# A spectral stage in a metaformer kernel: 33 of 64 frequency columns, four image pairs written out, loads placed ahead

## The reference

```python
x_proj = einsum('bchw,mc->bmhw', layernorm_over_channels(x), w_in)      # 16 channels
x_fft = fftshift(fft2(x_proj, norm='ortho'))
mag = abs(x_fft) + 1e-8
gain = einsum('ahw,cahw->chw', angle_weights, bin_weights[:, :, radius_idx])
enh = mag * gain * (cos(angle(x_fft)) + 1j * sin(angle(x_fft)))
x_enh = real(ifft2(ifftshift(enh), norm='ortho'))
x = x + layernorm_over_channels(x) + einsum('bmhw,cm->bchw', x_enh, w_out)
```

## Time and profile before

| what | value |
|---|---|
| median of 3 runs | 3474.5 us |
| lowest and highest | 3469.59 and 3474.97 us |
| the profiled execution | 3470.55 us |
| its span, first to last instruction | 3468.8 us |
| mean granted TensorE clock | 0.91 of full speed |
| TensorE / VectorE / ScalarE / GpSimd busy | 88% / 50% / 44% / 25% of the span |

### The profile page before, as it was taken

How to read it: one execution, slowest core, us unless ns; L and a number is a source line. 1 busy time by engine, 2 the same in 40 slices (tenths; PEclk the granted TensorE clock), 3 DMA queues, 4 the chain that set the end, 5 groups by cost and what they waited for, 6 DMA issues and landing times. The chain is left out here.

```text
span 3468.8 us, 66009 instructions
## 1 busy us (share of the span) xinstructions
PE 3045.2 (88%) x26432; PEld 1701.1 (49%) x26432; DVE 1727.8 (50%) x2317; ACT 1512.8 (44%) x2263; POOL 853.9 (25%) x694
## 2 busy tenths in 40 slices
PE   6766683899999975999998769999999999999989
PEld 1166321455555532566666234646454554646455
DVE  6724286577766440111111254656465555555575
ACT  4412351567677751111222344535454554545434
POOL 3500350344444421111110103121221213121322
PEclk7668675999999985999999789999999999999999
DMA  4611675123433324677777344655645564646244
GB/s 178 237 25 24 217 282 205 67 109 146 155 146 150 150 116 130 186 214 213 208 212 243 113 155 149 208 168 175 205 166 196 164 213 141 234 146 226 100 149 161
DMA packets 233863, 579.59 MB, mean 167 GB/s; under 512 B 38444, under 2 KB 105260, under 8 KB 225068
## 3 DMA queue, kind: packets, MB, share of 16 engines
q1 hardware_dynamic: 233684, 577.26, 49.8%
HBM read 384.24 MB, written 192.94 MB: 166 GB/s over the span
## 5 line engine op out<-in xcount | busy, mean ns | idle before, releaser
L2137 DVE TENSOR_TENSOR d_hid_scaled<-d_hid_scaled,d_gate 128x512 f32<-128x512 f32 x512 | 403.0, 799 | 437.1 <-PE d_ps L1835 266.2
L1835 PE MATMUL d_ps<-d_hid_scaled,d_w 128*128 128x512 f32 x1024 | 525.6, 595 | 4.3 <-DVE d_hid_scaled L2137 4.3
L1533 PE MATMUL c_ps<-c_pad,c_weight 32*32 32x512 f32 x13824 | 474.8, 601 | 26.1 <-ACT c_pad L1485 18.6
L2004 ACT ACTIVATE d_hid_scaled<-d_ps,d_b 128x512 f32<-128x512 f32 x512 | 349.7, 687 | 329.1 <-PE d_ps L1823 322.3
L1533 PEld LDWEIGHTS c_ps<-c_pad,c_weight 32*32 32x32 f32 x13824 | 287.0, 103 | 213.7 <-issue 129.4
L1821 PE MATMUL d_ps<-d_tnh,d_w1h 128*128 128x512 f32 x512 | 318.7, 623 | 19.8 <-ACT d_hid_scaled L2004 19.1
L1164 PE MATMUL b_ps<-b_hid,b_w2s 128*128 128x512 f32 x512 | 260.5, 593 | 0.0
L2089 POOL CAST d_tnh<-d_TN 128x512 fp32r<-128x512 f32 x64 | 47.3, 739 | 857.9 <-PE d_ps L1823 820.6
L1594 DVE COPY c_pad<-c_P 128x1024 f32<-128x1024 f32 x48 | 33.4, 696 | 414.5 <-PE c_ps L1533 379.2
L1485 ACT ACTIVATE c_pad<-c_P 128x1024 f32<-128x1024 f32 x48 | 51.8, 1079 | 392.2 <-PE c_ps L1533 372.0
L1835 PEld LDWEIGHTS d_ps<-d_hid_scaled,d_w 128*128 128x128 f32 x1024 | 194.4, 190 | 51.9 <-DVE d_hid_scaled L2137 5.7
(11 more groups left out here) (259 smaller groups left out, 5671.2 us busy)
## 6 DMA issues: line engine op xcount, KB each, us to landing
d_gate<-scratch_gates SPq DMA_DIRECT2D x256, 512.0 KB, 4.6
scratch_qkv<-b_qkv SPq DMA_DIRECT2D x64, 768.0 KB, 3.5
c_P<-scratch_qkv SPq DMA_DIRECT2D x192, 256.0 KB, 4.7
scratch_agg<-c_out SPq DMA_DIRECT2D x192, 256.0 KB, 4.9
d_buf<-scratch_qkv SPq DMA_DIRECT2D x96, 512.0 KB, 4.1
d_buf<-scratch_agg SPq DMA_DIRECT2D x96, 512.0 KB, 4.1
p_X<-in_x SPq DMA_DIRECT2D x8, 2048.0 KB, 8.4
scratch_s<-p_X SPq DMA_DIRECT2D x8, 2048.0 KB, 6.4
```

What stands on the lines that cost most here:

```text
L1533: end = nc.tensor.matmul(ps[on(i), k * QUADS + h, :].rearrange("p (b r w) -> p b r w", b=2, w=HB), weight[k][on(q), 2 * r + x, on(h)], pad ...
L1835: nc.tensor.matmul(moe_bank(n // E), w2[:, e, :], scaled[n % 3][:, :], start=False, stop=(e == E - 1)).then_inc(moe_pe, 1)
L2004: nc.scalar.activation(hid[n % 3][:, :], hid_bank(n), ACT.Gelu, bias=b1[:, n % E:n % E + 1]).then_inc(hid_done, 1)
L2137: nc.vector.tensor_tensor(scaled[n % 3][:, :], hid[n % 3][:, :], gate[k][:, n % 2 * CH:(n % 2 + 1) * CH], ALU.mult).then_inc(scaled_done, 1)
```

## The change

The spectrum of a real image is symmetric, so the column transform now makes 33 of the 64 columns (`KX`), the factors are computed for 33, and the last table of the inverse counts every column but the first and the last twice. The mask is made symmetric on the host to match. The transforms, and the copies `rows`, `back` and `image`, are cut into halves of 8 channels (`q`), with a wait for each half. The hardware loops are gone: the four pairs are written out. All four pairs of projections are loaded at the start of the stage, into four buffers; there are two image buffers. The gain matmuls come first in the stage. The tables are loaded in `phase_project`, behind the first four image loads.

```diff
+KX = SIDE // 2 + 1
+DFT_TABLES = ((0, 128), (128, 194), (194, 260), (260, 388), (388, 516), (516, 580), (580, 644))
...
@@ phase_project, SP, after the loads of images 0 to 3 @@
+                dft, mask, binw = early
+                for h in range(2):
+                    sp.dma_start(dft[h * SIDE:(h + 1) * SIDE, :], d["dft"]).then_inc(early_loaded, 16)
+                sp.dma_start(mask[:, :], d["mask"]).then_inc(early_loaded, 16)
+                sp.dma_start(binw[:, :], d["binw"]).then_inc(early_loaded, 16)
...
@@ phase_dft, SP @@
+                for i in range(STEPS):
                     for h in range(2):
-                        sp.dma_start(proj[h * SIDE:(h + 1) * SIDE, :, :],
-                                     d["pm"][bass.ds(i * 2 + h, 1), :, :].rearrange("a m (h w) -> h (a m) w", w=SIDE)).then_inc(pm_loaded, 16)
-                with sp.Fori(0, STEPS - 1) as i:
-                    sp.wait_ge(rows_pe, i + 1)
-                    load(i + 1)
-                    store(i)
-                store(STEPS - 1)
+                        sp.dma_start(proj[i][h * SIDE:(h + 1) * SIDE, :, :],
+                                     d["pm"][i * 2 + h:i * 2 + h + 1, :, :].rearrange("a m (h w) -> h (a m) w", w=SIDE)).then_inc(rest_loaded if i else first_loaded, 16)
+                for i in range(STEPS):
+                    sp.wait_ge(image_ready, i * 2 + 2)
...
@@ phase_dft, TensorE @@
-                    stage(high, 128, rows, [(g2a, 0), (g2b, SIDE)]).then_inc(freq_pe, 1)
+                    stage(high[:, q * 2 * CH:(q + 1) * 2 * CH], 128, rows, q, [(g2a, 0), (g2b, SIDE)]).then_inc(freq_pe, 1)
-                    stage(low, 128, enh, [(g3a, 0), (g3b, SIDE)]).then_inc(back_pe, 1)
+                    stage(wide(q), 128, enh, q, [(g3a, 0), (g3b, KX)], cols=KX).then_inc(back_pe, 1)
-                    stage(low, SIDE, back, [(g4a, 0), (g4b, SIDE)]).then_inc(image_pe, 1)
+                    stage(wide(q), SIDE, back, q, [(g4a, 0), (g4b, SIDE)], rows=KX).then_inc(image_pe, 1)
...
+                for i in range(STEPS):
+                    if i + 1 < STEPS:
+                        for q in range(2):
+                            by_columns(i + 1, q)
+                    for q in range(2):
+                        to_lines(i, q)
+                    for q in range(2):
+                        to_image(i, q)
+                    if i + 2 < STEPS:
+                        for q in range(2):
+                            by_rows(i + 2, q)
...
@@ phase_dft, ScalarE @@
+                copy_rows(0)
+                squares(0)
+                magnitude(0)
+                copy_rows(1)
+                for i in range(STEPS):
+                    if i + 1 < STEPS:
+                        squares(i + 1)
+                    copy_back(i, 0)
+                    if i + 1 < STEPS:
+                        magnitude(i + 1)
+                    copy_back(i, 1)
+                    for q in range(2):
+                        copy_image(i, q)
+                    if i + 2 < STEPS:
+                        copy_rows(i + 2)
```

More of the change, by code:

```diff
@@ L565, in _, with phase_dft @@
                 scale(B - 1, range(NCH))
-def phase_dft(nc, d, passed):
+def phase_dft(nc, d, tables):
+    dft, mask, binw = tables
     with ExitStack() as ctx:
@@ L577, in phase_dft @@
         low, high = ps[:, 0:4 * CH], ps[:, 4 * CH:8 * CH]
[L578 to L583, removed]
+        STEPS, HALF = B // 2, MID // 2
+        gain = sb("gain", [128, MID, KX])
+        proj = [sb(f"proj{i}", [128, MID, SIDE]) for i in range(STEPS)]
+        image = [sb(f"image{k}", [128, MID, SIDE]) for k in range(2)]
+        rows, back = [sb(n, [128, MID, 128]) for n in ("rows", "back")]
+        enh, sqz = [sb(n, [128, MID, 2 * KX]) for n in ("enh", "sqz")]
+        r2, mag, zero, den, rec, num, fac, shifted = [sb(n, [128, MID, KX]) for n in
                                                       ("r2", "mag", "zero", "den", "rec", "num", "fac", "shifted")]
[L585 to L588, removed]
+        g1, g2a, g2b, g3a, g3b, g4a, g4b = DFT_TABLES
+        first_loaded, rest_loaded, xe_stored = sem("first_loaded"), sem("rest_loaded"), [sem(f"xe_stored{k}") for k in range(2)]
         rows_pe, rows_ready, freq_pe, sqz_done, r2_done, mag_done, enh_ready = [sem(n) for n in
@@ L623, in _, with stage @@
+                for k in range(2):
+                    sp.wait_ge(xe_stored[k], STEPS // 2 * 32)
             @block.tensor
             def _(pe):
[L625 to L631, removed]
+                def stage(dst, width, src, q, tables, rows=SIDE, cols=SIDE):
+                    for m in range(HALF):
+                        for t, (g, first) in enumerate(tables):
@@ L644, in by_columns @@
-                def by_columns(i):
-                    pe.wait_ge(rows_ready, i + 1)
+                                on = slice(h * SIDE, h * SIDE + rows)
+                                last = nc.tensor.matmul(dst[h * SIDE:h * SIDE + cols, m * width:m * width + g[1] - g[0]],
+                                                        src[on, q * HALF + m, first:first + cols], dft[on, g[0]:g[1]],
+                                                        start=(t == 0), stop=(t == len(tables) - 1))
@@ new lines, in stage, with by_rows @@
+                    return last
+                def by_rows(i, q):
+                    if i == 0:
+                        pe.wait_ge(first_loaded, 32)
+                    else:
+                        pe.wait_ge(rest_loaded, (STEPS - 1) * 32)
+                    if i == 1:
+                        pe.wait_ge(rows_ready, q + 1)
+                    if i >= 2:
+                        pe.wait_ge(image_ready, (i - 2) * 2 + q + 1)
+                    stage(wide(q), 128, proj[i], q, [(g1, 0)]).then_inc(rows_pe, 1)
@@ L661, in _ @@
                 for h in range(2):
-                    for kx in range(SIDE):
+                    for kx in range(KX):
                         last = nc.tensor.matmul(high[h * SIDE:(h + 1) * SIDE, kx * MID:(kx + 1) * MID],
                                                 mask[:, kx * SIDE:(kx + 1) * SIDE], binw[:, :], start=True, stop=True)
[L665 to L671, removed]
@@ L672, in _ @@
-                inverse(STEPS - 1)
+                last.then_inc(rows_pe, 1)
+                for i in range(2):
+                    for q in range(2):
+                        by_rows(i, q)
+                    if i == 0:
+                        for q in range(2):
+                            by_columns(0, q)
+                for i in range(STEPS):
[7 more added lines that the diff above has]
+                    if i + 2 < STEPS:
+                        for q in range(2):
+                            by_rows(i + 2, q)
@@ L674, in _, with copy_rows @@
             @block.scalar
             def _(act):
[L676 to L682, removed]
+                def copy_rows(i):
+                    for q in range(2):
+                        act.wait_ge(rows_pe, i * 2 + q + 2)
+                        nc.scalar.activation(of_half(rows, q), wide(q), ACT.Copy).then_inc(rows_ready, 1)
@@ L683, in forward, with squares, magnitude @@
+                def squares(i):
+                    act.wait_ge(freq_pe, i * 2 + 2)
+                    nc.scalar.activation(sqz[:, :, :], z[:, :, 0:2 * KX], ACT.Square).then_inc(sqz_done, 1)
+                def magnitude(i):
                     act.wait_ge(r2_done, i + 1)
                     nc.scalar.activation(flat(mag), flat(r2), ACT.Sqrt).then_inc(mag_done, 1)
[L686 to L697, removed]
+                def copy_back(i, q):
+                    act.wait_ge(back_pe, i * 2 + q + 1)
+                    nc.scalar.activation(of_half(back, q), wide(q), ACT.Copy).then_inc(back_ready, 1)
+                def copy_image(i, q):
+                    act.wait_ge(image_pe, i * 2 + q + 1)
+                    if i >= 2:
+                        act.wait_ge(xe_stored[i % 2], i // 2 * 32)
+                    nc.scalar.activation(of_half(image[i % 2], q), wide(q)[:, 0:HALF * SIDE], ACT.Copy).then_inc(image_ready, 1)
@@ L699, in _ @@
             @block.vector
             def _(dve):
[L701 to L705, removed]
+                dve.wait_ge(rows_pe, 1)
+                nc.vector.tensor_copy(gain[:, :, :], high[:, 0:KX * MID].rearrange("p (x m) -> p m x", m=MID)).then_inc(enh_ready, 1)
```

79 lines of the change are left out of this document (38 added, 41 removed).

## The result

The changed kernel takes 3377.05 us in the median of 4 runs (3374.29 to 3378.99), the kernel before 3472.48 in the median of 4 (3469.59 to 3474.97): a ratio of 0.9727, with a 95% interval of 0.9709 to 0.9745. The forecast was 3386.5, between 3374 and 3410.

What follows compares the result with a forecast made beforehand. A chain handing work between engines, none full, was taken as the bound. The stage ends at 283.0 instead of 371.0, 88.0 us earlier, less 2 set aside for clock drops: 3384.5; half the runs' 4.0 offset added: 3386.5, range 3374 to 3410.

Steps and rivals of the forecast that it cites:

- The gain: First in the spectral stage: 66 matmuls at clock 0.50 take 13.5 us; 6.6 us is the low bound at clock 1.00.
- The loads: Eight projection loads at the stage's start finish behind the gain; TensorE's 42.1 us of waits go, tables cost nothing.
- Rows(0), cold, 6.4: First pair's row transforms, right after the gain, run at a cold clock and take 6.4 us.
- Columns at 66: Column transforms narrowed from 128 to 66 wide take 4.05 us, 0.063 a matmul, bounds 3.95 and 7.16.
- 33-wide tiles: Inverse transforms on 33-wide tiles keep their times: 7.16 us to lines, 3.95 us to image.
- Rivals 2 and 4: Inverse halves run serially: at full clock 3431 us, chance 0.04; at clock 0.50 slower than before, 3507 us, chance 0.03.
- VectorE at 528: VectorE's chain of eight operations at width 528 takes 8.3 us instead of 14.8, its reciprocal 3.45.
- The third rival: VectorE's chain stays long because runs of 33 cost as 64 did: 23.4 us more, 3410 us; chance 0.05.
- Rounds of 19.2: Transforms of a pair's round sum to 18.8 us plus 0.4 for hand-overs; round 0 adds 2.0 for a cold start.
- TensorE bounds the rounds by a little: In the rounds VectorE's path needs 17.9 us against TensorE's 19.2, a margin of 1.3 us.
- The first rival: TensorE's clock stays at 0.50 through rounds 0 to 3, costing 42 us: 3427 us; chance 0.06.
- Round 3: Last pair's inverse only: 7.16 + 3.95 + 0.2 us, ending at 277.0, then a 0.7 us last copy.

Runs made afterwards that it cites:

- e4_loads: Changed kernel with only the first two projection pairs loaded at the start, later pairs issued behind stores; stage 129.8 us, time 3398.95 us.
- e3_tables: Changed kernel with its four table loads back at the start of the spectral stage, ahead of the projections; stage 114.1 us, time 3381.87 us.
- e6_gain: Changed kernel with the gain's 66 matmuls alternating between the two halves instead of one half after the other; stage 101.2 us, time 3368.58 us.
- e5_root: Changed kernel with the next pair's square root moved ahead of the first back copy on ScalarE; stage 102.9 us, time 3368.01 us.
- e1_full: Changed kernel with all 64 columns, only the half spectrum undone; stage 167.8 us, time 3438.24 us.
- e2_half: Kernel before with 33 columns only, keeping its loop, loads, tables and order; stage 163.4 us, time 3438.82 us.
- e9_whole: Changed kernel with each transform waiting for both halves of the copy ahead, not only its own; stage 123.0 us, time 3393.29 us.

## Why the prediction was right

It was right in sign and mechanism, and the time lies inside the range; the forecast was 9.4 us too long. By its own steps, each length from the stage's start on:

- **The gain**, 13.5 us first in the stage: 13.51. The bound of 6.6 was not met, the clock stood at 0.50.
- **The loads** hidden: no wait for projections. e4_loads brings 18.0 us of waits back, e3_tables 7.3 for the tables. That eight loads at once do not hold up the first pair, which the forecast took, is right: in e6_gain it is there 7.2 us after the stage's start.
- **Rows(0), cold, 6.4**: 4.9 from 181.94 to 186.84, 1.5 us less. The granted clock was 0.50 from 181 to 185 and 0.99 from 185 to 187; in the cold row transforms of before it was 0.50 from 184 to 187 and still 0.60 from 187 to 190.
- **Columns at 66**: 3.91, which is 0.061 a matmul, or 0.059 by the 3.75 us from start to start. The line between the widths had 0.063, so the measurement is with the rows. The Trainium skill (TensorEngine Tiling (Array Packing), Instruction Overhead) gives each matmul about 60 cycles of overhead; the estimate from that, added to the width, was 0.070, and the trace does not agree with that estimate.
- **33-wide tiles** as 64-wide ones: 7.17 and 3.91. Rivals 2 and 4 fall with these two rows.
- **VectorE at 528**: reciprocal 3.45, as worked out; from the square's start to the next columns 11.15 us (11.0 forecast from the columns' end). The third rival falls.
- **Rounds of 19.2**: 18.0. This is the mis-sized term: I summed the transforms' own durations and added 0.4 for hand-overs, but a transform starts before the one ahead of it has drained (239.56 + 3.93 is 243.49, and the next began at 243.31), so the steps are 3.75, 6.99, 3.73 and 3.50. Round 0 took 19.6, round 1 18.0, 2.8 us less together.
- **TensorE bounds the rounds by a little**: shown by e5_root, where a root 2.6 us earlier in the round leaves the rounds as they are. The margin was smaller than the forecast's 1.3: VectorE's last product ended at 239.02, 0.5 us before the columns of 239.56. The first rival falls with the clock of 1.00 from 206 to 256.
- **Round 3** was 1.0 us longer than forecast: the last inverse started cold (8.64) behind its 2.9 us wait. The 2 us set aside for drops of the clock cover it.
- **The project stage**: 3.8 us that no step had; at least 2.2 of them are scatter (e3_tables), and no run points to another cause for the rest.

The stage came to 107.0 where the sum had 110.8 before the 2 us set aside. So of the 10.2 us between the sum's 3384.5 and the profiled 3374.29, the stage makes 3.8, the amount set aside 2.0, the project stage 3.8 and what lies behind 0.7, all to the same side. The range's lower end was worked out from a gain at full clock and no cold start, and neither came; that the time still lies 3 us inside it is in part luck.

What the forecast had not said is that its parts do not add: it never asked what each would bring alone, and e1_full and e2_half show that over a quarter of the gain exists only with both.

## What to carry to other kernels

Where a stage is a chain between engines, read the wait that ends last in each round and ask what is next when it goes: halving one engine's work brings little while the wait for a load fills the same time (2.0 and 1.3 us a round for the narrow spectrum behind the old loads), and loading ahead leaves the long chain as the next wait (6.4 us a round in e1_full). The gain's two tiles of the array overlapped only when their matmuls alternated in program order, so try the loop over tiles inside. Cutting copies into halves can be worth more than the wait it removes: in e9_whole the gaps cost the clock as well.

## What had not been expected of the hardware

In e9_whole gaps of 0.8 to 1.1 us between transforms were followed by a granted clock of 0.50 and rows of 5.36 and 6.56 us, though TensorE had been busy for most of the time ahead (10.95 of the 13 us from 230 to 243); in the kernel before, 2.06 us gaps at the same place left 3.95 us image transforms at the high clock three times (262.22, 302.28, 360.69) and once not (339.47, 5.50 us), and in e2_half they took 4.8 to 4.9 us behind such gaps all four times. Which gap costs the clock could not be told from its length in these runs.

Eight projection loads issued in a row took SP 10.88 us. The first three took 0.64 to 0.67 us each, the other five 1.30 to 2.83. Two in a row took 1.37 and 1.43 us together in the trace of before (at 174.47 and 190.43), and 2.25 and 2.20 behind stores (269.56 and 309.58). What made the later issues long is not shown. In the changed kernel no engine waited for SP then.
